# Graph network with four propagation sweeps: identity added on VectorE in sweep 4, half groups spaced 16 substeps, last half group finished in quarters

## The reference

```python
h = maximum(ln(x), 0); x = x + (adj/rowsum) @ h @ W_in + (adj.T/colsum) @ h @ W_out
h = maximum(ln(x), 0); x1 = silu(adj @ h @ W + b); x = x + silu(adj @ x1 @ W + b)
h = maximum(ln(x), 0); A = adj + eye; s = rsqrt(A.sum(1)); x = x + relu((s*A*s) @ h @ W + b)
h = maximum(ln(x), 0); A = adj + eye; s = rsqrt(A.sum(1)); x = x + relu((s*A*s) @ (h @ W) + b)
```

## Time and profile before

| | |
|---|---|
| median of 3 runs | 1154.41 us (1153.81 to 1154.59) |
| the profiled execution | 1153.61 us, of which the span is 1151.8 us |
| PE / PEld busy | 97% / 80% |
| DVE busy | 91% |
| ACT busy | 79% |
| granted PE clock | 0.999 over the span |
| transfers | 355 GB/s mean, 407 MB |
| chain that ended last | PE 83%, DVE 10%, ACT 4% |

### The profile page before, as it was taken

One profiled execution on the slowest core, in us unless ns is written; L12 is line 12 of the kernel. 1 busy time (PEld: TensorE's weight loads), 2 busy tenths in 40 slices (PEclk: granted clock), 3 DMA queues, 4 the chain that ended last, 5 costly groups with the idle time before them and its releaser, 6 DMA issues.

```text
span 1151.8 us, 14790 instructions
## 1 busy us (share of the span) xinstructions
PE 1120.3 (97%) x5120; PEld 919.1 (80%) x5120; DVE 1046.6 (91%) x1419; ACT 909.1 (79%) x1265; POOL 48.0 (4%) x40
## 2 busy tenths in 40 slices
PE   4999999999999899999999999999999999999997
PEld 3778888888876678888888887888888888888886
DVE  5999989989899999987988999999999999998985
ACT  6888897887777868787887787888777788776772
POOL 0000000000000000000000211201112111000000
PEclk9999999999999999999999999999999999999999
DMA  9999999999988889999999999999999999998984
GB/s 348 339 337 394 391 410 377 352 407 381 341 301 304 300 282 400 401 381 362 396 346 381 312 383 332 369 379 340 376 340 358 379 327 376 353 394 331 401 330 171
DMA packets 113546, 408.36 MB, mean 355 GB/s; under 512 B 12608, under 2 KB 13632, under 8 KB 113472
## 3 DMA queue, kind: packets, MB, share of 16 engines
q1 hardware_dynamic: 113472, 407.42, 95.1%
HBM read 405.27 MB, written 2.10 MB: 354 GB/s over the span
## 4 chain that ended last, share of the span: by engine, by line
PE 83%; DVE 10%; ACT 4%; issue 2%; DMA 0%; ACTq 0%; DVEq 0%
PE bank L604 52%; PE bank L608 27%; DVE a_lo L385 6%; PE bank L615 3%; ACT a_hi L270 3%; PE bank L636 1%; ACT act_raw L294 1%; DVE x_sb L482 1%; DVE h_lo L408 1%; DVE zt L390 1%; DVE stats L415 0%; ACT a_hi L268 0%; DMA x_sb<-in_x_dram 0%; DVE zt L394 0%; DVE mv L419 0%
## 5 line engine op out<-in xcount | busy, mean ns | idle before, releaser
L385 DVE TENSOR_TENSOR a_lo<-raw,a_hi 128x1024 fp32r<-128x1024 f32 x768 | 898.3, 1219 | 64.7 <-ACT a_hi L268 49.9
L268 ACT ACTIVATE a_hi<-raw 128x1024 fp32r<-128x1024 f32 x512 | 520.6, 1054 | 81.1 <-DMA raw<-in_adj_t_dram 65.5
L604 PE MATMUL bank<-a_hi,h_hi 128*128 128x512 f32 x1536 | 480.0, 394 | 14.6 <-ACT a_hi L270 14.5
L608 PE MATMUL bank<-a_lo,h_hi 128*128 128x512 f32 x1536 | 479.1, 393 | 9.3 <-DVE a_lo L385 7.7
L604 PE MATMUL bank<-a_hi,h_lo 128*128 128x512 f32 x1536 | 474.6, 390 | 0.0
L608 PEld LDWEIGHTS bank<-a_lo,h_hi 128*128 128x128 f32 x1536 | 285.0, 188 | 85.8 <-DVE a_lo L385 28.6
L604 PEld LDWEIGHTS bank<-a_hi,h_hi 128*128 128x128 f32 x1536 | 284.2, 188 | 72.7 <-DVE h_lo L408 14.5
L604 PEld LDWEIGHTS bank<-a_hi,h_lo 128*128 128x128 f32 x1536 | 288.9, 188 | 61.4
L270 ACT ACTIVATE a_hi<-raw 128x1024 fp32r<-128x1024 f32 x256 | 269.7, 1055 | 29.4 <-DMA raw<-in_adj_dram 8.5
L303 ACT ACTIVATE act_raw<-x_sb,lnbias,lnscale 128x128 f32<-128x128 f32 x96 | 39.7, 484 | 47.0 <-DVE lnbias L443 47.0
L252 POOL TENSOR_TENSOR std<-mv,eps_sb 128x4 f32<-128x4 f32 x16 | 17.4, 1088 | 931.6 <-DVE mv L419 931.6
(11 more groups left out here) (50 smaller groups left out, 183.4 us busy)
## 6 DMA issues: line engine op xcount, KB each, us to landing
raw<-in_adj_t_dram SPq DMA_DIRECT2D x640, 512.0 KB, 6.5
raw<-in_adj_dram SPq DMA_DIRECT2D x128, 512.0 KB, 6.3
x_sb<-in_x_dram SPq DMA_DIRECT2D x4, 512.0 KB, 10.5
out_dram<-x_sb SPq DMA_DIRECT2D x8, 256.0 KB, 7.0
w_sb<-in_L_gnn_W_dram SPq DMA_DIRECT2D x3, 64.0 KB, 11.3
b_sb<-in_L_gnn_b_dram SPq DMA_DIRECT2D x3, 64.0 KB, 8.1
w_sb<-in_L_gnn_W_in_dram SPq DMA_DIRECT2D x1, 64.0 KB, 12.3
w_sb<-in_L_gnn_W_out_dram SPq DMA_DIRECT2D x1, 64.0 KB, 12.3
```

Source lines behind the costliest of these rows:

```text
L268: act.activation(sub(a_hi, n), sub_raw(n), ACT.Copy).then_inc(sub_hi, 1)
L385: dve.tensor_tensor(sub(a_lo, n), sub_raw(n), sub(a_hi, n).bitcast(F32), ALU.subtract).then_inc(sub_lo, 1)
L604: pe.matmul(bank[half][:, :], weights, hi_a[:, half * GW:(half + 1) * GW], start=start and weights is hi_w, stop=False)
L608: last = pe.matmul(bank[half][:, :], hi_w, lo_a[:, half * GW:(half + 1) * GW], start=False, stop=stop)
```

## The change

1. In sweep 4 the identity product on PE is gone. In its place DVE adds the 128 x 128 identity to the diagonal block of the 8 tiles of each group that hold one (s = 8g to 8g+7), in place in `raw`, before ACT splits the tile. The add for tile n+2 stands ahead of `lo(n)` in DVE's list and waits for that tile's transfer; `hi` of that tile waits for the add. Sweep 3 keeps the product on PE.
2. `LATER` goes from 8 to 16: half 1 of a finished group is handled 16 substeps after half 0. While g = 0 it stays 8.
3. The last four substeps run bank by bank: all 12 matmuls of half 0, then those of half 1. Half 0 is multiplied by W after two substeps of half 1.
4. The very last half goes through ACT, PE, DVE and the store in two quarters of 256 columns, in two different banks.

```diff
+        PLUS_AHEAD = 2
+        plus_cols = {}
+        plus_n = {}
+        for g in range(NG):
+            for b in range(CB):
+                n = n_of(SWEEPS, g, g * CB + b)
+                plus_n[n] = len(plus_cols)
+                plus_cols[n] = slice(b * P, (b + 1) * P)
...
-        LATER = 8
+        LATER, LATER_FIRST = 16, 8
...
-        def late(at, s):
-            return [h for h in range(2) if at is not None and at + h * LATER == s]
+        def late(at, g, s):
+            return [h for h in range(2) if at + h * (LATER if g else LATER_FIRST) == s]
...
             def hi(n, accum=None):
                 act.wait_ge(tile_in[n % RAWS], 16 * (n // RAWS) + 16)
+                if n in plus_cols:
+                    act.wait_ge(plus_ready, plus_n[n] + 1)
...
-            for half in range(2):
-                prod_out(SWEEPS, NG - 1, half)
+            act.wait_ge(tail_ready, 1)
+            act.wait_ge(z_ready, z_of(SWEEPS, NQ - 2) - 1)
+            act.activation(prod_t[:, 0, :], out_ps[(NG - 1) % 2][0][:, :], ACT.Copy).then_inc(prod_ready, 1)
+            act.wait_ge(tail_ready, 2)
+            act.wait_ge(z_ready, z_of(SWEEPS, NQ - 1) - 1)
+            for quarter in range(2):
+                cols = slice(quarter * GW // 2, (quarter + 1) * GW // 2)
+                act.activation(prod_t[:, 1, cols], out_ps[(NG - 1) % 2][1][:, cols], ACT.Copy).then_inc(prod_ready, 1)
...
+            def plus(n):
+                block = sub_raw(n)[:, plus_cols[n]]
+                if plus_n[n] == 0:
+                    dve.wait_ge(ident_made, 2)
+                dve.wait_ge(tile_in[n % RAWS], 16 * (n // RAWS) + 16)
+                dve.tensor_tensor(block, block, ident[:, :], ALU.add).then_inc(plus_ready, 1)
+
             def lo(n):
+                if n + PLUS_AHEAD in plus_cols:
+                    plus(n + PLUS_AHEAD)
...
-            for half in range(2):
-                z_out(SWEEPS, 2 * (NG - 1) + half)
+            z_out(SWEEPS, NQ - 2)
+            for quarter in range(2):
...
+                dve.wait_ge(z_ready, zi + 1 + quarter)
...
+                for b in (2 * quarter, 2 * quarter + 1):
+                    ins = dve.scalar_tensor_tensor(out=zt[:, b * D:(b + 1) * D], in0=quarter_ps[quarter][:, b * D:(b + 1) * D],
...
+                dve.scalar_tensor_tensor(out=x_sb[:, blocks, :], in0=zt[:, cols].rearrange("p (b f) -> p b f", b=2),
+                                         scalar=0.0, in1=x_sb[:, blocks, :], op0=ALU.max, op1=ALU.add).then_inc(x_upd, 1)
...
-                        if sweep >= 3 and s == AT_OWN:
+                        if sweep == 3 and s == AT_OWN:
                             identity_product(sweep, g, bank)
...
             for half in range(2):
-                finish(SWEEPS, NG - 1, half)
+                for s in range(NS - TAIL, NS):
+                    tail_products(n_of(SWEEPS, NG - 1, s), hi_set[:, s, :], lo_set[:, s, :], bank, half, s == NS - 1)
+                    if half == 1 and s == NS - TAIL // 2 - 1:
+                        finish(SWEEPS, NG - 1, 0)
+            for quarter in range(2):
+                finish_quarter(quarter)
```

More of the change, by code:

```diff
@@ L31, in build_gnn_stack @@
     SWEEPS = 4
+    TAIL = 4
     RING = 8
@@ L232, in _ @@
                 load_tile(n)
-            for q in range(NQ):
+            for q in range(NQ - 1):
                 sp.wait_ge(x_upd, 2 * NQ + q + 1)
                 sp.dma_start(out[:, GB * q:GB * q + GB, :], x_sb[:, GB * q:GB * q + GB, :]).then_inc(out_done, 16)
-            sp.wait_ge(out_done, 16 * NQ)
+            for quarter in range(2):
+                blocks = slice(GB * NQ - GB + 2 * quarter, GB * NQ - GB + 2 * quarter + 2)
+                sp.wait_ge(x_upd, 3 * NQ + quarter)
+                sp.dma_start(out[:, blocks, :], x_sb[:, blocks, :]).then_inc(out_done, 16)
+            sp.wait_ge(out_done, 16 * (NQ + 1))
         @block.gpsimd
@@ L579, in _ @@
                             continue
-                        for half in late(AT_Z, s):
+                        for half in late(AT_Z, g, s):
                             z_out(ps, 2 * pg + half)
                         if ps in (2, 3):
-                            for half in late(AT_STATS, s):
+                            for half in late(AT_STATS, g, s):
                                 if ps == 2:
@@ L587, in _ @@
                                 ln_stats(ps, 2 * pg + half)
[L588 removed]
+                            for half in late(AT_AFFINE, g, s):
                                 ln_affine(ps, 2 * pg + half)
                         if ps in (1, 2, 3):
[L591 removed]
+                            for half in late(AT_LO[ps], g, s):
                                 split_lo(ps, 2 * pg + half)
[L593 to L594 removed]
+            z_out(SWEEPS, NQ - 2)
+            for quarter in range(2):
+                zi = z_of(SWEEPS, NQ - 1)
+                blocks = slice(GB * NQ - GB + 2 * quarter, GB * NQ - GB + 2 * quarter + 2)
+                cols = slice(quarter * GW // 2, (quarter + 1) * GW // 2)
+                dve.wait_ge(z_ready, zi + 1 + quarter)
+                if quarter == 0:
+                    dve.wait_ge(x_upd, 3 * NQ - 1)
+                for b in (2 * quarter, 2 * quarter + 1):
+                    ins = dve.scalar_tensor_tensor(out=zt[:, b * D:(b + 1) * D], in0=quarter_ps[quarter][:, b * D:(b + 1) * D],
+                                                   scalar=d_isqrt[:, GB * NQ - GB + b:GB * NQ - GB + b + 1],
+                                                   in1=b_sb[:, B_OF[SWEEPS], :], op0=ALU.mult, op1=ALU.add)
+                ins.then_inc(zt_ready, 1)
+                dve.wait_ge(zt_ready, zi - 16 + 1 + quarter)
+                dve.scalar_tensor_tensor(out=x_sb[:, blocks, :], in0=zt[:, cols].rearrange("p (b f) -> p b f", b=2),
+                                         scalar=0.0, in1=x_sb[:, blocks, :], op0=ALU.max, op1=ALU.add).then_inc(x_upd, 1)
         @block.tensor
@@ L609, in products, with tail_products @@
                 last.then_inc(sub_used, 1)
+            def tail_products(n, hi_w, lo_w, bank, half, stop):
+                cols = slice(half * GW, (half + 1) * GW)
+                pe.wait_ge(sub_hi, n + 1)
+                for weights in (hi_w, lo_w):
+                    pe.matmul(bank[half][:, :], weights, sub(a_hi, n)[:, cols], start=False, stop=False)
+                pe.wait_ge(sub_lo, n + 1)
+                last = pe.matmul(bank[half][:, :], hi_w, sub(a_lo, n)[:, cols], start=False, stop=stop)
+                if stop:
+                    last.then_inc(tail_ready, 1)
             def weight_product(zi, half, src, w):
@@ L629, in finish, with finish_quarter @@
                 weight_product(z_of(sweep, 2 * g + half), half, prod_t[:, half, :], W_OF[sweep])
+            def finish_quarter(quarter):
+                zi = z_of(SWEEPS, NQ - 1)
+                pe.wait_ge(prod_ready, prod_of(SWEEPS, NQ - 1) + 1 + quarter)
+                if quarter == 0:
+                    pe.wait_ge(zt_ready, zi - 2 - 16 + 1)
+                for b in (2 * quarter, 2 * quarter + 1):
+                    last = pe.matmul(quarter_ps[quarter][:, b * D:(b + 1) * D], prod_t[:, 1, b * P:(b + 1) * P],
+                                     w_sb[:, W_OF[SWEEPS], :], start=True, stop=True)
+                last.then_inc(z_ready, 1)
             def identity_product(sweep, g, bank):
@@ L677, in _ @@
                             pe.wait_ge(h_ready, split_n(sweep - 1, s // GB) + 1)
+                        if sweep == SWEEPS and g == NG - 1 and s >= NS - TAIL:
+                            continue
                         products(n_of(sweep, g, s), hi_set[:, s, :], lo_set[:, s, :], bank, s == 0, s == NS - 1)
-                        if sweep >= 3 and s == AT_OWN:
+                        if sweep == 3 and s == AT_OWN:
                             identity_product(sweep, g, bank)
```

9 lines of the change are left out of this document (6 added, 3 removed).

## The result

| | before | after |
|---|---|---|
| median of 6 runs each, us | 1153.66 (1152.61 to 1154.59) | 1145.12 (1144.76 to 1145.57) |
| the profiled execution / its span, us | 1153.61 / 1151.8 | 1145.57 / 1143.6 |

After against before: 0.9926, with a 95% interval of 0.9916 to 0.9937, which is 8.5 us less; 1145.4 was forecast, as 9.1 us less than a median of 1154.41.

A forecast was written before the change was run, and what follows sets the result against it. PE was taken as the bound (97% busy, 83% of the chain), with DVE nearly level wherever a layer norm is under way. -7.36 + 1.7 - 1.4 - 2.0 = -9.1 us gave 1145.4 us against the median, range 1142.4 to 1149.7.

The forecast's parts named there:

- Identity off PE, -7.36: Sweep 4: four identity products of 1.84 us leave PE, with PE the pace in all four groups: -7.36 us.
- The price of an add: DVE in sweep 4: an add lasts 0.28 us and takes 0.20 us from DVE, between 0.07 and 0.26.
- Free in groups 1 to 3: Sweep 4: DVE needs 41.2 us against PE's 45.34, so adds cost nothing; without that cover, 4.8 us.
- Group 0 of sweep 4, +1.7: DVE also carries sweep 3's last layer norm there; lead 3.8 less 5.5 makes PE wait 1.7 us, between 0.8 and 3.3.
- so s = 5 still reaches about 5.1: Sweep 3 groups, new spacing: lead (end of `lo` to PE's first matmul on that tile) at s = 5 is about 5.1 us.
- and almost wholly given back: Sweep 4, group 0: the identity product's 1.84 us is won, but PE waits 1.7 us.
- Spacing, -1.4: Sweeps 2 and 3, spacing 16: PE's waits fall from 3.23 to 1.8 us, -1.4; bounds -3.2 and +0.4.
- Waiting for the tile two ahead costs nothing.: Sweep 4, groups 1 to 3: the add's wait costs nothing, as DVE ends the sweep 7.8 us ahead of PE.
- The end, -2.0: Kernel's end: 8.5 us after the last matmul becomes 6.5, counting 0.92 of moved weight products: -2.0, between -1.2 and -2.5.
- A: Rival, 8%: DVE keeps up everywhere, the spacing removes every wait, also in sweep 4's group 0: -12.6, 1141.8 us.
- B: Rival, 20%: the spacing costs; +1.8 in place of -1.4, and +2.7 in place of +1.7 in sweep 4: 1149.5 us.
- C: Rival, 3%: the adds break the run-ahead, a substep with an add takes 2.6 us in place of 1.36: 1168 us.

The follow-up runs named there:

- e7: Kernel after, with a second, useless add ahead of each of the 8 adds of sweep 4's group 0: 1146.88 us, ratio 0.9944 to before.
- e8: Kernel after, with a second, useless add ahead of each of the 24 adds of sweep 4's groups 1 to 3: 1145.38 us, ratio 0.9931 to before.
- e1: Kernel before, with only the spacing of 16 substeps (`LATER`) added: 1152.43 us against 1153.67, ratio 0.9988.
- e4: Kernel after, but group 0 of sweep 4 keeps its identity product on PE and has no adds: 1144.39 us, ratio 0.9920 to before.
- e9: Kernel after, with the 32 adds on GpSimd in place of DVE: 1145.43 us, ratio 0.9923 to before.
- e10: Kernel after, with each add one tile ahead of its `lo` in place of two: 1145.62 us, ratio 0.9927 to before.
- e5: Kernel after, with spacing 8 everywhere, adds and new end kept: 1145.79 us, ratio 0.9927 to before.
- e3: Kernel before, with only the adds on DVE in sweep 4, old spacing and old end: 1148.12 us, ratio 0.9952 to before.
- e2: Kernel after without the adds and with spacing 8, so only the end differs from before: 1151.64 us, ratio 0.9984 to before.
- e11: Kernel after, spacing 16 behind sweeps 1 and 2, 8 behind 3 and 4; sweep 4 group 0: half 0 adds on DVE, half 1 product on PE: 1144.24 us.

## Why the prediction was right, point by point

The total was right to 0.3 us, and that closeness is partly luck. The forecast was 9.1 us less than before; 8.2 us less is measured in the spans and 8.5 in the medians. What closed the gap is that the 9.1 were taken from a median of three runs, 1154.41, and the median of six is 1153.66. Of the terms, the wait in group 0 was forecast 1.3 us too small, and the gains of the spacing and of the end 0.2 us too small each. The bounds of the terms add up to 1142.2 and 1149.6, where 1142.5 and 1148.5 are printed; the measured time lies well inside either.


- **Identity off PE, -7.36.** Confirmed: groups 1 and 2 of sweep 4 take 45.33 us, to the hundredth what was worked out.
- **The price of an add.** 283 ns measured, 0.28 forecast; 0.20 us taken from DVE, as forecast (950.31 - 950.11). e7 gives the same 0.20 us an extra add in group 0, below the 0.28 that the prediction drew from the Trainium skill ("VectorE: DVE Perf Modes", "The DRAIN you can't avoid"). It quoted only half of that section, which goes on to say that a next op which isn't held (one that needn't wait for all earlier ones to finish) starts earlier. The trace agrees with that half: the next instruction starts 0.08 us ahead of the recorded end. **Free in groups 1 to 3**: shown by e8.
- **Group 0 of sweep 4, +1.7.** It was +2.97, inside the bounds of 0.8 to 3.3. The mechanism was right (lead at s = 5 less what is lost to s = 23), and so was the loss, 30.00 - 24.49 = 5.51 us for 5.50; 0.2 us of waits just behind s = 23 came on top. The step that was off is "so s = 5 still reaches about 5.1": the lead at s = 5 of sweep 3, group 3 was 4.06, and the missing 1.0 us was carried unchanged to s = 5 of sweep 4 (2.79 for 3.8; at s = 0 it was 0.86 for 2.1). The balance behind that step held: DVE was to gain 47.18 - 47.03 = 0.15 us a group, and the leads at s = 5 of sweep 3's groups 1 to 3 after were 3.77, 3.91 and 4.06. What I had not seen is that 0.15 us a group refills nothing. After the wait in group 0 of sweep 3, the lead is set once, by when the transfers land at the start of group 1, and then hardly changes. ACT's rows at s = 2, s = 3 and from s = 5 of that group in the kernel after:

```profile
810.59 1.06 ACT L290 ACTIVATE a_hi<-raw 128x1024 fp32r<-128x1024 f32 x1 [1.92 <-DMA raw<-in_adj_t_dram]
811.85 1.06 ACT L290 ACTIVATE a_hi<-raw 128x1024 fp32r<-128x1024 f32 x1 [0.20 <-DMA raw<-in_adj_t_dram]
...
814.72 2.04 ACT L290 ACTIVATE a_hi<-raw 128x1024 fp32r<-128x1024 f32 x2
```

ACT stands 1.92 us for the tile of s = 2 and 0.20 for that of s = 3; behind that it runs without a stop through the splits of s = 3 and 4 and two copies of finished banks, and DVE follows it. The tile of s = 5 had been there for 0.33 us (814.39) when ACT came to it, so it is not this tile that set the lead. Seven kernels have the same instructions up to there (after, e1, e4, e7, e8, e9, e10). At s = 1 their leads are 3.20 to 3.25; at s = 5 they are 3.77, 5.09, 4.61, 4.27, 4.43, 4.49 and 4.31. What lies between is the landing of the tile of s = 3, which comes 2.71 us behind the start of `lo` at s = 1 in the kernel after and 1.14 to 2.22 in the others; in the six that stay below 5.1, this time and the lead at s = 5 sum to 6.47 to 6.52. In e4 it then goes 4.61, 4.77, 4.92; in e8 4.43, 4.57, 4.71. So 5.1 was the most it could be, reached in one of seven. The prediction did hold this case among its bounds, as transfers that land late (a lead 1.2 us short), but not in the forecast.
- **Its product won "and almost wholly given back".** More than wholly: e4, which leaves it on PE, has a group 0.4 to 1.1 us shorter (against e8 and the kernel after). Even entered with the full lead of 5.08, group 0 with its adds would take, by my estimate, 45.33 + 5.76 - (5.08 - 1.27) = 47.3 us, no less than the 47.18 with the product.
- **Spacing, -1.4.** -1.6 in the windows of the whole change; -1.4 between the averages of four and seven kernels; e1 alone -1.2 us. The places were nearly right too: the last waits at sweep 2, group 3 (0.72 us, 0.3 forecast) and sweep 3, group 0 (0.95, 1.5 forecast; the lead at s = 5 was 3.35, 2.8 forecast), nothing before and behind. Whether the spacing keeps this worth once the adds are in isn't settled: e5 (8) and the kernel after (16) end within 0.7 us of each other, but e5 had the fewest waits in sweeps 2 and 3 of the four with spacing 8. The old spacing does bring more lead to sweep 4, of which the wait for a landing takes a part.
- **"Waiting for the tile two ahead costs nothing."** True for groups 1 to 3 and for the kernel after. With spacing 8 DVE stands 1.27 us (e5) and 1.90 us (e3) at the first add.
- **The end, -2.0.** -2.2 in e2, and -4.01 + 1.84 = -2.2 in the windows. Of the steps, the last bank matmul to the end was forecast 5.6 and is 5.4 us: a copy of 256 columns 0.39 (0.38), four matmuls 0.73 (0.62), two scaled additions 0.62 (0.61), the last of 256 columns 0.42 (0.43), the store 2.1 (2.3).
- **Rivals.** A (no wait left) is out by the 0.72, 0.95 and 2.97 us; B (the spacing costs) by e1; C (the adds break the run-ahead) by groups 1 and 2 of sweep 4, which take 45.33 us with eight adds each.

## What to carry to other kernels

Where two engines are nearly level, don't ask which is busier: take the lead of one over the other at a fixed place in each stretch, add up what each stretch uses and refills, and put the wait where the sum goes below zero. Work moved off the bound engine is won only in stretches where the receiving engine has lead to spare; in the one stretch without, it is no worse left where it is, and by the windows better (e4, e11). A wait that stands ahead of unrelated work in an engine's list, as the add for tile n+2 ahead of `lo(n)`, is costly just when that engine is well ahead of the transfers.

## What was not expected of the hardware

- Transfers of the same 512 KB tiles, in the same order, land differently from one execution to the next. They mostly land 1.28 us apart, but with gaps: from s = 1 to s = 2 of sweep 3 group 1 it was 2.98 us in the kernel after and 1.57 in e1. This shifts the lead by up to 1.3 us (3.77 to 5.09 at one place in seven kernels with the same instructions up to there), and one window, sweep 2 group 3, took 47.40 us in e8 and 46.05 to 46.10 in the other kernels with spacing 16 there. So single profiles of this kernel can't attribute less than about 1 us by their totals. Why the landings differ stays open.
- A 128-column add takes 0.46 us on GpSimd alone, 283 ns on DVE. Beside DVE's `lo` instructions its record grows to 0.95 to 1.44 us, which is waiting for DVE, and it makes the next `lo` 0.27 us longer, about the length of the same add on DVE.
- 24 extra DVE instructions, 6.8 us of work at 283 ns, cost 0.06 us where PE is the pace.
